# Attention stacks loaded in place by DMA, an opening in halves, and other lags in the stream of heads

## The reference

```python
x = x + 0.5 * ffn0(layernorm(x))
x = x + attn0(layernorm(x))
x = x + 0.5 * ffn0(layernorm(x))
x = x + 0.5 * ffn1(layernorm(x))
x = x + attn1(layernorm(x))
x = x + 0.5 * ffn1(layernorm(x))

# attn1: 16 heads of 16 features, sequences of 256
c_kv = h @ w_dkv.T
q = (h @ w_q.T).reshape(B, S, 16, 16)
k = (c_kv @ w_uk.T).reshape(B, S, 16, 16)
v = (c_kv @ w_uv.T).reshape(B, S, 16, 16)
scores = einsum("bqhd,bkhd->bhqk", q, k) / 4 + alibi_bias    # causal
out = einsum("bhqk,bkhd->bqhd", softmax(scores), v)
return out.reshape(B, S, 256) @ w_o.T
```

## Time and profile before

| what | value |
|---|---|
| median of 3 runs | 552.72 us (550.92 to 553.23) |
| the profiled execution's own time | 550.05 us |
| its span, first to last instruction | 548.3 us |
| TensorE busy | 500.9 us (91%) |
| VectorE busy | 390.5 us (71%) |
| ScalarE busy | 264.2 us (48%) |
| GpSimd busy | 126.5 us (23%) |
| mean granted TensorE clock | 0.978 |

### The profile page before, as it was taken

One profiled execution on the slowest core, in us unless ns is written; L12 is line 12 of the kernel. 1 busy time (PEld: TensorE's weight loads), 2 busy tenths in 40 slices (PEclk: granted clock), 3 DMA queues, 4 the chain that ended last, 5 costly groups with the idle time before them and its releaser, 6 DMA issues.

```text
span 548.3 us, 9179 instructions
## 1 busy us (share of the span) xinstructions
PE 500.9 (91%) x3074; PEld 424.8 (77%) x3074; DVE 390.5 (71%) x1196; ACT 264.2 (48%) x572; POOL 126.5 (23%) x201
## 2 busy tenths in 40 slices
PE   1999999999999999999999995898779978889996
PEld 1788888888888888888888885787566766668885
DVE  3669787764786863986597778787479777637776
ACT  2657543433334343235454352465558766544441
POOL 1001000110200100100010043358146545414342
PEclk9999999999999999999999997999879999889999
DMA  6332210000000000001100000700737320000011
GB/s 200 105 98 82 92 40 1 0 1 1 2 1 0 2 0 1 2 1 59 48 11 2 0 2 0 203 0 1 220 111 256 107 79 2 1 0 2 1 39 39
DMA packets 16734, 24.83 MB, mean 45 GB/s; under 512 B 2736, under 2 KB 11184, under 8 KB 16592
## 3 DMA queue, kind: packets, MB, share of 16 engines
q1 hardware_dynamic: 15632, 23.73, 14.2%
q10 hardware_dynamic: 1056, 0.51, 0.3%
HBM read 18.99 MB, written 5.24 MB: 44 GB/s over the span
## 4 chain that ended last, share of the span: by engine, by line
PE 80%; DVE 7%; ACT 5%; issue 5%; POOL 2%; DMA 1%; ACTq 1%; DVEq 0%; POOLq 0%
PE ps L575 22%; PE ps L577 21%; PE ps L576 21%; DVE x L1597 2%; PE ps L893 2%; PE ps L590 2%; PE ps L860 2%; PE ps L877 2%; ACT z L1002 2%; PE ps L879 1%; PE ps L848 1%; PE ps L966 1%; DMA post_b<-in_posts_dram 1%; ACT qs L1211 1%; DVE tmp L1440 1%
## 5 line engine op out<-in xcount | busy, mean ns | idle before, releaser
L575 PE MATMUL ps<-zh,w0u_h 128*128 128x512 f32 x256 | 102.8, 401 | 2.5 <-issue 2.5
L577 PE MATMUL ps<-zl,w0u_h 128*128 128x512 f32 x256 | 102.2, 399 | 0.0
L576 PE MATMUL ps<-zh,w0u_l 128*128 128x512 f32 x256 | 101.8, 398 | 0.0
L1032 ACT ACTIVATE gel<-ps 128x512 f32<-128x512 f32 x64 | 38.2, 597 | 103.9 <-PE ps L577 103.8
L1415 DVE TENSOR_TENSOR act<-gel,ps 128x512 f32<-128x512 f32 x64 | 43.7, 683 | 42.9 <-ACT gel L1032 42.7
L575 PE MATMUL ps<-w0d_h,ah 128*128 128x256 f32 x256 | 73.0, 285 | 0.4
L577 PE MATMUL ps<-w0d_l,ah 128*128 128x256 f32 x256 | 71.4, 279 | 0.0
L576 PE MATMUL ps<-w0d_h,al 128*128 128x256 f32 x256 | 71.4, 279 | 0.0
L508 POOL TENSOR_TENSOR al<-act,ah 128x512 fp32r<-128x512 f32 x32 | 42.4, 1327 | 83.8 <-ACT ah L1109 83.6
L1597 DVE SCALAR_TENSOR_TENSOR x<-ps,aff,x 128x256 f32<-128x256 f32 x128 | 53.0, 476 | 9.9 <-PE ps L577 8.2
L1038 ACT ACTIVATE ah<-act 128x512 fp32r<-128x512 f32 x64 | 40.3, 629 | 40.2 <-DVE act L1415 40.2
(11 more groups left out here) (183 smaller groups left out, 1085.2 us busy)
## 6 DMA issues: line engine op xcount, KB each, us to landing
stage<-in_w_dram SPq DMA_DIRECT2D x16, 384.0 KB, 3.0
q_raw<-split_out SPq DMA_DIRECT2D x24, 128.0 KB, 2.7
k_raw<-split_out SPq DMA_DIRECT2D x48, 64.0 KB, 2.4
stage<-in_w_dram SPq DMA_DIRECT2D x8, 256.0 KB, 2.6
k_raw<-in_zeros_dram SPq DMA_DIRECT2D x1, 1536.0 KB, 11.1
x<-in_x_dram SPq DMA_DIRECT2D x2, 512.0 KB, 5.3
split_out<-qh SPq DMA_DIRECT2D x4, 256.0 KB, 2.4
split_out<-ql SPq DMA_DIRECT2D x4, 256.0 KB, 2.7
```

What stands on the lines that cost most here:

```text
L575: pe.matmul(o, lh, rh, start=start, stop=False, **kw)
L576: pe.matmul(o, ll, rh, start=False, stop=False, **kw)
L577: return pe.matmul(o, lh, rl, start=False, stop=stop, **kw)
L1032: nc.scalar.activation(gel[:, n % 2, :], ps[:, 2 * (n % 2), :], ACT.Gelu_apprx_tanh).then_inc(gelu_s, 1)
```

## The change

- Stacks: `q_raw` and `k_raw` are gone, and `qs` and `ks` have 16 places for 8. `read` writes straight into them, four halves in rotation; a half is overwritten when the transposed scores of all its eight heads are done. The copies of ScalarE (`round_q`) and GpSimd (`round_pair`) are gone, and `scores` waits for the DMAs of its half.
- Zeros and constants of `ks`: GpSimd sets 16 partitions of a new tile `pad` to zero in ffn1, ScalarE rounds the constant rows into it once (32x512), and seven DMAs on SP spread both over the 16 places: six of 256 KB, one of 1 MB.
- Opening: the first block of x comes in two DMAs, and the statistics of its first two tiles wait for the first only. The wait for the constants and the small product move behind TensorE's second unit.
- Halves, in every block: transposes, `z_hi` and `z_lo` signal each of the two halves of z by itself, so that the second half is transposed while the first is rounded. The matmuls still wait for both.
- Stream: TURN 7, SUM 14, OUT_STEPS (28, 30, 33, 35, 37, 39). In a step TensorE does `scores_t` ahead of `shift_turn`; ScalarE does `out_hi` first; VectorE does `out_lo` one step after `out_turn` for two. V_STEPS, LN_STEPS and Z_STEP stay.

The diff, cut to what the steps above touch:

```diff
@@ -53,16 +53,16 @@
 GROUP = 4
-TURN = 6
-SUM = 12
-OUT_STEPS = (27, 29, 32, 34, 36, 38)
+TURN = 7
+SUM = 14
+OUT_STEPS = (28, 30, 33, 35, 37, 39)
 V_STEPS = (25, 41)
...
 HALF = PAIRS // 2
-SLOTS = 8
-AHEAD = 6
+SLOTS = 16
 STACKED = 16 * 9
+HALVES = SLOTS // HALF
@@ -385,8 +384,11 @@
             def load_x(b):
-                sp.dma_start(x[:, BT * b:BT * (b + 1), :],
-                             x_in[BLK * b:BLK * (b + 1), :].rearrange("(t p) d -> p t d", p=P)).then_inc(x_in_s[b], 16)
+                parts = 1 if b else 2
+                for i in range(parts):
+                    lo, hi = BT * b + BT * i // parts, BT * b + BT * (i + 1) // parts
+                    sp.dma_start(x[:, lo:hi, :], x_in[P * lo:P * hi, :].rearrange("(t p) d -> p t d", p=P))\
+                      .then_inc(x_in_s[2 * i + b], 16)
@@ -400,14 +402,14 @@
             def read(h):
-                n, m, i = h // 2, h % 2, h % 2
+                n, m, i = h // 2, h % 2, h % HALVES
                 b, cols, rows = n // 2, slice(n % 2 * SEQ, (n % 2 + 1) * SEQ), slice(P * m, P * (m + 1))
-                if h >= 2:
-                    sp.wait_ge(pair_s, HALF * (h - 1))
-                    sp.wait_ge(q_pair_s, HALF * (h - 1))
+                slots = slice(HALF * i, HALF * (i + 1))
+                if h >= HALVES:
+                    sp.wait_ge(t_ps, 2 * HALF * (h - HALVES + 1))
                 sp.wait_ge(written_s[0][m], 32 * (b + 1))
                 for part, hl in enumerate((0, 1, 0)):
-                    sp.dma_start(q_raw[PAIR * part:PAIR * (part + 1), i, :, :],
+                    sp.dma_start(qs[PAIR * part:PAIR * (part + 1), slots, :].bitcast(F32),
                                  split_out[0, hl, b, rows, cols].rearrange("(a r) q -> r a q", r=PAIR))\
@@ -415,7 +417,7 @@
                         r = PAIR * part + HD * e
-                        sp.dma_start(k_raw[r:r + HD, i, :, e, :], src[e]).then_inc(stack_s[i], 16)
+                        sp.dma_start(ks[r:r + HD, slots, e, :].bitcast(F32), src[e]).then_inc(stack_s[i], 16)
@@ -431,9 +433,18 @@
                 sp.dma_start(rows_raw, rows_in).then_inc(sel_in_s, 16)
-                sp.dma_start(k_raw[0:K_ROWS, :, :, :, :].rearrange("p i a e q -> p (i a e q)"),
-                             zeros_in.partition_broadcast(K_ROWS)).then_inc(zero_s, 16)
-                sp.wait_ge(zero_s, 16)
+                sp.wait_ge(pad_zero_s, 1)
+                for part in range(3):
+                    for e in range(2):
+                        r = PAIR * part + HD * (1 - e)
+                        sp.dma_start(ks[r:r + HD, :, e, :].bitcast(F32),
+                                     pad[0:HD, 0:SEQ].bitcast(F32).rearrange("p (o q) -> p o q", o=1)
+                                     .broadcast_to([HD, SLOTS, SEQ])).then_inc(zero_s, 16)
+                sp.wait_ge(rows_s, 1)
+                sp.dma_start(ks[K_ROWS:P, :, :, :].rearrange("p s e q -> p s (e q)").bitcast(F32),
+                             pad[K_ROWS:P, :].bitcast(F32).rearrange("p (o q) -> p o q", o=1)
+                             .broadcast_to([P - K_ROWS, SLOTS, 2 * SEQ])).then_inc(pad_s, 16)
+                sp.wait_ge(zero_s, 6 * 16)
                 for m, kind in ((0, 0), (1, 0), (0, 1), (1, 1)):
@@ -502,6 +513,10 @@
                     slot = (U0 * f0 + n) % NA
+                    if n == U1 and "attn1" in stages:
+                        for i in range(2):
+                            pool.wait_ge(x_s[i], last_ffn0 + 1)
+                        nc.gpsimd.memset(pad[0:HD, :].bitcast(F32), 0.0).then_inc(pad_zero_s, 1)
                     pool.wait_ge(ah1_s, n + 1)
@@ -551,11 +558,7 @@
                         ln_scale(st.p + 1)
-                        for gp in range(AHEAD):
-                            round_pair(gp)
                         for hd in range(4 * HEADS):
-                            if hd % 2 == 0 and hd // 2 + AHEAD < 4 * PAIRS:
-                                round_pair(hd // 2 + AHEAD)
                             if hd == LN_STEPS[0] - TURN + 1:
@@ -589,7 +592,7 @@
                                           ident[:, :])
-                mm.then_inc(zt_s, 1)
+                    mm.then_inc(zt_s, 1)
@@ -625,8 +628,8 @@
             def split_ready(p):
-                pe.wait_ge(zh_s, zt_count(p))
-                pe.wait_ge(zl_s, zt_count(p))
+                pe.wait_ge(zh_s, KC * zt_count(p))
+                pe.wait_ge(zl_s, KC * zt_count(p))
@@ -650,6 +653,10 @@
                             logits_t(0, 6, fb == 0)
+                        if fb == 0 and c == 1:
+                            pe.wait_ge(const_s, 16 * N_SETUP)
+                            pe.matmul(ps[0:SA, 7, 0:SA], a0[:, 2 * SA:3 * SA], a0[:, SA:2 * SA], start=True, stop=True)\
+                              .then_inc(pt_ps_s, 1)
                         if c == 3:
@@ -765,11 +772,11 @@
                         scores(s)
+                    if TURN <= s < 4 * HEADS + TURN:
+                        scores_t(s - TURN)
                     if s % GROUP == 1 and GROUP < s < 4 * HEADS + GROUP:
                         shift_turn(s // GROUP - 1)
-                    if TURN <= s < 4 * HEADS + TURN:
-                        scores_t(s - TURN)
-                    if s % GROUP == 0 and s >= SUM:
+                    if s >= SUM and (s - SUM) % GROUP == 0:
                         for c in range(2):
@@ -835,8 +842,9 @@
                 if e == 0:
-                    pe.wait_ge(pair_s, gp + 1)
-                    pe.wait_ge(q_pair_s, gp + 1)
+                    if gp % HALF == 0:
+                        h = gp // HALF
+                        pe.wait_ge(stack_s[h % HALVES], STACKED * (h // HALVES + 1))
                     if gp == 0:
@@ -865,7 +873,7 @@
                 if hd == 0:
-                    pe.wait_ge(rows_s, 2)
+                    pe.wait_ge(pad_s, 16)
                     pe.wait_ge(qh_s, 3)
@@ -967,10 +975,6 @@
-            if "attn0" in stages:
-                pe.wait_ge(const_s, 16 * N_SETUP)
-                pe.matmul(ps[0:SA, 7, 0:SA], a0[:, 2 * SA:3 * SA], a0[:, SA:2 * SA], start=True, stop=True)\
-                  .then_inc(pt_ps_s, 1)
             for st in plan:
@@ -997,17 +1001,16 @@
                 act.wait_ge(shift_z_s, p - BY_ACT + 1)
-                act.wait_ge(zt_s, zt_count(last_norm(p)))
+                act.wait_ge(zt_s, KC * zt_count(last_norm(p)))
                 for t in range(BT):
...
             def z_hi(p):
-                act.wait_ge(zt_s, zt_count(p))
                 for kc in range(KC):
-                    a = nc.scalar.activation(zh[:, kc, :], ps[:, kc, :], ACT.Copy)
-                a.then_inc(zh_s, 1)
+                    act.wait_ge(zt_s, KC * (zt_count(p) - 1) + kc + 1)
+                    nc.scalar.activation(zh[:, kc, :], ps[:, kc, :], ACT.Copy).then_inc(zh_s, 1)
@@ -1118,12 +1121,9 @@
                             nc.scalar.activation(wa_h[:, :], wa_raw, ACT.Copy).then_inc(wah_s, 1)
-                        if fb == 1 and c in (4, 5) and "attn1" in stages:
+                        if fb == 1 and c == 4 and "attn1" in stages:
                             act.wait_ge(sel_in_s, 32)
-                            slots = slice((c - 4) * SLOTS // 2, (c - 3) * SLOTS // 2)
-                            nc.scalar.activation(ks[K_ROWS:P, slots, :, :].rearrange("p s e q -> p s (e q)"),
-                                                 rows_raw.rearrange("p (o q) -> p o q", o=1)
-                                                 .broadcast_to([P - K_ROWS, SLOTS // 2, 2 * SEQ]), ACT.Copy).then_inc(rows_s, 1)
+                            nc.scalar.activation(pad[K_ROWS:P, :], rows_raw, ACT.Copy).then_inc(rows_s, 1)
@@ -1165,27 +1165,21 @@
                 k_hi(1, 0)
-                for gp in range(2):
-                    round_q(gp)
                 q_hi(1, 1)
                 k_hi(1, 1)
-                for gp in range(2, AHEAD):
-                    round_q(gp)
                 for s in range(4 * HEADS + SUM):
+                    for n in range(3):
+                        for t in range(2):
+                            if s - HEADS * n == OUT_STEPS[3 * t + 1] + 1:
+                                out_hi(n, t)
                     if s % GROUP == 1 and GROUP < s < 4 * HEADS + GROUP:
...
                         probs(s - TURN)
-                        if s % 2 == 0 and (s - TURN) // 2 + AHEAD < 4 * PAIRS:
-                            round_q((s - TURN) // 2 + AHEAD)
                     if s == LN_STEPS[1]:
                         normalise(p + 2)
-                    if s % GROUP == 1 and s > SUM:
+                    if s > SUM and (s - SUM) % GROUP == 1:
                         out_t((s - SUM) // GROUP)
-                    for n in range(3):
-                        for t in range(2):
-                            if s - HEADS * n == OUT_STEPS[3 * t + 1] + 1:
-                                out_hi(n, t)
                     if s - 1 in V_STEPS:
@@ -1293,6 +1278,8 @@
```

(11 more changed lines are left out.)

35 lines of the change are left out of this document (9 added, 26 removed).

## The result

| | before | after |
|---|---|---|
| median of the runs | 552.46 us (550.92 to 553.23, 4 runs) | 537.73 us (537.07 to 538.21, 4 runs) |
| the profiled execution's own time | 550.05 us | 537.07 us |
| its span | 548.3 us | 535.3 us |
| mean granted TensorE clock | 0.978 | 0.979 |

A forecast was written before the change was run, and what follows sets the result against it. TensorE, 80% of the chain that ended last, was taken as the bound, with gains only where it waits. -2.0 - 2.0 - 5.5 - 0.3 = -9.8 gave 540.3 from 550.05 or 542.9 from 552.72; 541.5 was predicted, range 535 to 549.

The forecast's parts named there:

- Opening: Start of the kernel: x in two pieces, later constants' wait and halves of z give -2.0 us (bounds -1.0 and -2.6).
- Entry: Entry into attn1 (372 to 400 us): without the second constant-row fill, transposes stop waiting; -2.0 us (-1.4 and -2.7).
- The fill: Seven SP DMAs of zeros and constant rows before the first write of q: about 20 us, hidden, priced at nothing.
- Stream: The 64 heads of attn1 (400 to 471 us): new lags and removed copies give -5.5 us (0 and -9).
- plain group: Stream group of four heads without v or output steps: 3.95 us falls to 3.45, -1.5 for three.
- group with v: First group of four heads in the stream that has v work: -0.4 us.
- Stacks by DMA: Stream scores wait for a half's nine transfers instead of casts; eighteen steps cover them, priced at nothing.
- Tail: End of attn1 (471 to 490 us): extra head and sums against earlier out_hi, about even; -0.3 us (+1.5 and -2).
- full gain: Rival: lower-clock stretches in the stream's first groups and tail shrink too; stream and tail -9.5, 538 us; chance 0.17.
- Lockstep: Rival: in the stream DVE and TensorE take back each other's gains; stream only -1.5, about 545.5 us; chance 0.25.
- even: Rival: moved stream steps cost what they give, only opening and entry remain; 550 to 553 us; chance 0.08.
- late fill: Rival: zeros and constant rows land late, the first write of q waits; about 568 us; chance 0.03.

The follow-up runs named there:

- e5_opening_alone: The kernel before with only x in two pieces, the halves of z and the later constants' wait; 549.93 us, ratio 0.9959.
- e7_second_fill: The changed kernel with two idle ScalarE copies of 32x1024 put back where the removed second constant-row fill stood; 539.04 us, ratio 0.9763.
- e1_old_lags: The changed kernel with the old lags and order (TURN 6, SUM 12, old output steps), stacks by DMA kept; 543.88 us, ratio 0.9869.
- e11_sum12: The changed kernel with only SUM back at 12; TURN 7 and the order of steps stay; 547.00 us, ratio 0.9897.
- e2_lags_alone: The kernel before with the new lags and order alone; stacks, casts, opening and entry as before; 544.47 us, ratio 0.9881.
- e8_quarters: The changed kernel with ScalarE's tail normalisation of four tiles done one tile per step at steps 61 to 64; 534.58 us, ratio 0.9664.
- e3_pool_copies: The changed kernel with 32 idle GpSimd casts of 96x512 put back at their old places; 537.22 us, ratio 0.9738.
- e10_best: The changed kernel with the tail normalisation one tile per step and 30 idle matmuls ahead of the first transposes; 532.42 us, ratio 0.9634.

## Why the prediction was right, and where it wasn't

**What bounds the kernel** was read rightly: nothing changed but the four stretches where TensorE waited.

**Opening, -2.0 forecast, -1.2 in this execution.** The milestones came as worked out: transposes at 8.95 (9.1 was said), first matmul at 12.37 (12.5). In this execution the fast rate came at 17.96, near the 18.64 of before, the early matmuls ran slowly, and the gain was near the lower bound. That was this execution's luck: the fast rate came at 15.32 to 18.41 in the ten traces with the changed opening, at 18.61 and 18.64 in the two with the old one, and the gain at the first router product was 1.8 us on average (1.0 to 2.5). With the 2.08 of e5_opening_alone's medians, -2.0 was well placed.

**Entry, -2.0 forecast, -2.4 measured.** Transposes without a wait, statistics 3.32 earlier (2.2 and the opening's part), the next transposes 3.47 earlier, and e7_second_fill brought 1.5 of the loss back when the second copy came back. What makes up the other 0.9 no run separates.

**The fill** was priced at nothing, and rightly. It was sized at about 20 us; from the first issue (349.55) to the last landing (373.91) it took 24, and the zeros, which are what the first write waits for, 19. The Trainium skill (SBUF — State Buffer, Door 1: The DMA port swizzle) gives 104 GB/s for partitions 0 to 15 and 189 for 0 to 31: this trace shows 92 and 191 for transfers to 16 and 32 partitions, within an eighth of the page.

**Stream, -5.5 forecast, -7.1 measured** (turn 0 to turn 14) between two executions with the same 6.83 us at the half level. In the five other traces of this stream a longer stretch at the half level takes 1.5 to 2.0 us of it back (-5.1 to -5.6). The forecast had neither this loss nor the 1.6 us by which the gain at like clock is larger, so that these traces come near 5.5 is partly luck. The plain group was said to fall to 3.45 and fell to 3.39: -1.7 for three, -1.5 forecast. The group with v gave 0.65 (0.4 forecast), the two cycles with output steps 2.16 and 1.77 (1.7 each), the two groups before them 0.84 (0.2). The mechanism of the lags stands: e1_old_lags and e11_sum12 take the sums away from behind the turn, and the group is 3.95 and 4.18. The sizes inside the group: the lags give -0.4 (3.95 to about 3.55) where -0.45 was forecast. The shift steps fall from 1.0 us to 0.34, where 0.4 to 0.8 was forecast, and the group gains 0.14 to 0.20 by that and by the waits that went with the copies. What the prediction didn't see is that the second counts only on top of the first. With the old lags the turn, the shift copy and the next scores follow each other in a ring of 3.95 us, and a faster DVE changes nothing in it; only the groups with v or output steps gained from the stacks then, 1.6 us together.

The Trainium skill (SBUF — State Buffer, Who interferes with whom) says that a DVE instruction with two SBUF inputs contends with a GpSimd instruction that reads SBUF. The trace bears this out for the casts (168 ns without them, 394 with them); that the masks would still cost up to 0.8 per group, as I read the page for the prediction, didn't happen in the changed kernel's plain groups, where both steps take 0.17. GpSimd's masks end at 415.06 there, both steps begin at 415.20 and 415.40, and the next mask only at 415.46: it comes later and holds up nothing. Masks do hold a step up where they meet it: no cast is left in e1_old_lags and e11_sum12, and yet in each of their plain groups one step that runs beside masks takes 0.38 to 0.41 us. So the masks cost nothing here because of when they come, and a shift of 0.2 us in the program could change that.

**Stacks by DMA, nothing forecast, about -1.1.** I asked only whether the scores would wait for a transfer, not what else waited for one. ScalarE's `round_q` did, with the copy of the sums behind it; the row stands in e2_lags_alone. With the old lags most of it is hidden: the first group with v gains 0.28 us from the stacks in e1_old_lags, and 1.40 with the new lags.

**Tail, -0.3 forecast, -2.3 measured.** This is the term that was mis-sized most. I set the earlier `out_hi` (0.5 to 0.9) against one more head and group of sums to do (1.17). But the wait for `out_lo` went altogether, 1.8 us, and the wait behind the norm didn't grow (1.63 after 1.8). e2_lags_alone has the same tail without the stacks, so it is the lags' alone. Most of the 2.3 is the clock. The windows from 455 to 500 us, before, after and e8_quarters:

```profile
455.00:500.00 45.00, 37.60 (x305) 30.04 (x298) 25.96 (x127) 24.09 (x58) 16.27 (x35) 0.92 0.01 1
```

```profile
455.00:500.00 45.00, 40.89 (x310) 33.86 (x309) 29.58 (x120) 23.76 (x53) 18.19 (x30) 0.96 0.01 1
```

```profile
455.00:500.00 45.00, 41.30 (x325) 34.21 (x323) 30.56 (x124) 25.66 (x57) 18.57 (x31) 1.00 0.00 1
```

A mean granted clock of 0.92, 0.96 and 1.00 over 45 us comes from two stretches of 3.41 us at the half level (1.2 GHz), one and none. One such stretch costs 1.54 us here (16.91 in the changed kernel, 15.37 in e3_pool_copies without one). Two taken from 19.21 leave about 16.1, an estimate, against 15.37: without the clock the tail gains some 0.8 us, where 0.3 was forecast, and the stretch that went gives the other 1.5. A wait of 1.8 us of TensorE is followed within 0.9 us by such a stretch in all six cases in the tails of the kernel before, e5_opening_alone and e1_old_lags, though not after the wait of 1.78 in the stream of e2_lags_alone; one of 1.63 within 1.7 us in seven of eight traces, with e3_pool_copies the exception; and without that wait (e8_quarters, e10_best) there is none. So the waits and the stretches go together in the tail, but not without exception. With the old lags and without casts (e1_old_lags) the windows of 470 to 480 and 480 to 490 both read 0.83, as before; with the new ones alone only the first does. The prediction had this as its rival "full gain" (stream and tail -9.5, 538, chance 0.17), and named the gap of 1.81 in front of such a stretch as what speaks for it. Stream and tail gave -9.4: the rival's number came, and its mechanism in the tail. In the stream's first groups it didn't: 6.83 us at the half level both before and after. So what the term for the tail had wrong is that it priced the moved work alone and put the clock at nothing.

**Lockstep, even and late fill** didn't come. Plain groups under 3.9 and a first write that waits for nothing were the marks named against them.

What stays open: what places the half-level stretches. Who is first in ffn1, how long the start of the stream takes and what the tail costs go with them, and no run here moves one of them by itself.

## What to carry to other kernels

When engines hand a small result round in a ring (turn, copy, next product), put work that depends on none of it right behind the hand-over; a faster engine elsewhere in the ring is worth nothing to the ring until that is done. Edits can be worth more together than one by one (here 1.6 and 2.9 us of the stream alone, 6.3 together), so price them in both orders. Compare traces group by group, and look where the clock's half level lies in each, before a stretch's length is called the same. When a copy goes, ask also what it waited for and what was queued behind it. Split a long piece of ScalarE work that nobody needs at once, when what stands behind it frees a buffer for TensorE.
